# Two groups of transposes become one, ahead of a tile's scores: attention and soft-dispatch block on one core

## The reference

```python
q = rope(jnp.einsum('bim,mhd->bhid', x, wq))
k = rope(jnp.einsum('bim,mhd->bhid', x, wk))
v = jnp.einsum('bim,mhd->bhid', x, wv)
s = jnp.einsum('bhid,bhjd->bhij', q, k) / 128
p = jax.nn.softmax(s - 1e30 * (i < j), axis=-1)
o = jnp.einsum('bhij,bhjd->bhid', p, v)
x = layernorm(x + jnp.einsum('bhid,hdm->bim', o, wo))
x = layernorm(x + slot_ffn(x))
```

## Time and profile before

| | |
|---|---|
| median of 3 runs | 1807.03 us (1807.0 to 1810.64) |
| profiled execution, its own time | 1805.92 us |
| its span, first to last instruction | 1803.9 us |
| mean granted TensorE clock | 0.977 |
| TensorE busy | 1702.5 us, 94% |
| VectorE busy | 1439.6 us, 80% |
| ScalarE busy | 1238.1 us, 69% |
| GpSimd busy | 1132.2 us, 63% |

### The profile page before, as it was taken

How to read it: one execution, slowest core, us unless ns; L and a number is a source line. 1 busy time by engine, 2 the same in 40 slices (tenths; PEclk the granted TensorE clock), 3 DMA queues, 4 the chain that set the end, 5 groups by cost and what they waited for, 6 DMA issues and landing times. The chain is left out here.

```text
span 1803.9 us, 33428 instructions
## 1 busy us (share of the span) xinstructions
PE 1702.5 (94%) x10524; PEld 1482.8 (82%) x10524; DVE 1439.6 (80%) x2947; ACT 1238.1 (69%) x2362; POOL 1132.2 (63%) x696
## 2 busy tenths in 40 slices
PE   4999999999999999999999999999999965999997
PEld 3788888888888888888888888888888854889986
DVE  3888988897899888978998889788989955677764
ACT  2777777776777777767777777777777732565563
POOL 3556666665666666656666666666666624677775
PEclk7999999999999999999999999999999987999998
DMA  3222232223222323232223223322222212123212
GB/s 105 71 71 74 76 98 69 73 76 89 66 78 71 103 64 79 75 85 70 75 76 106 63 78 79 91 71 71 71 82 72 71 64 71 48 55 92 64 30 53
DMA packets 76678, 134.23 MB, mean 74 GB/s; under 512 B 19296, under 2 KB 45920, under 8 KB 76512
## 3 DMA queue, kind: packets, MB, share of 16 engines
q1 hardware_dynamic: 75328, 131.15, 27.1%
q10 hardware_dynamic: 1184, 1.05, 0.2%
HBM read 56.36 MB, written 8.70 MB: 36 GB/s over the span
## 5 line engine op out<-in xcount | busy, mean ns | idle before, releaser
L454 ACT ACTIVATE probs<-ps_slot,neg_max 128x640 f32<-128x640 f32 (+7 forms) x512 | 378.6, 741 | 123.9 <-DVE neg_max L540 114.5
L540 DVE CUSTOM_DVE_ANT_0 ps_slot<-ps_slot,causal 128x640 f32<-128x640 f32 (+7 forms) x512 | 387.1, 756 | 52.0 <-PE ps_slot L57 50.4
L691 PE MATMUL ps_turn<-ident,probs 128*128 128x128 f32 x2304 | 340.4, 277 | 18.5 <-DVE x_t L597 6.2
L418 POOL TENSOR_TENSOR q<-rot_q,q 128x1024 fp32r<-128x1024 f32 x64 | 153.9, 2405 | 240.5 <-ACT q L471 240.5
L691 PEld LDWEIGHTS ps_turn<-ident,probs 128*128 128x128 f32 x2304 | 256.5, 141 | 53.4 <-DVE x_t L597 7.9
L55 PE MATMUL ps_slot<-k,q 128*128 128x512 f32 (+3 forms) x768 | 283.9, 370 | 2.2 <-DVE rot_q L556 1.3
L57 PE MATMUL ps_slot<-k,q 128*128 128x512 f32 (+3 forms) x768 | 266.2, 347 | 0.0
L56 PE MATMUL ps_slot<-k,q 128*128 128x512 f32 (+3 forms) x768 | 266.1, 347 | 0.0
L410 POOL TENSOR_TENSOR swapped_q<-swapped_q,rope 128x1024 f32<-128x1024 f32 x64 | 165.7, 2589 | 76.0 <-DMA swapped_q<-unrot_q 76.0
L418 POOL TENSOR_TENSOR k<-rot_k,k 128x1024 fp32r<-128x1024 f32 x64 | 153.1, 2392 | 85.8 <-ACT k L471 84.2
L410 POOL TENSOR_TENSOR swapped_k<-swapped_k,rope 128x1024 f32<-128x1024 f32 x64 | 153.5, 2399 | 55.9 <-DMA swapped_k<-unrot_k 55.8
(11 more groups left out here) (159 smaller groups left out, 4360.0 us busy)
## 6 DMA issues: line engine op xcount, KB each, us to landing
swapped_k<-unrot_k SPq DMA_DIRECT2D x128, 256.0 KB, 3.6
swapped_q<-unrot_q SPq DMA_DIRECT2D x128, 256.0 KB, 3.7
inv_b<-inv_rows SPq DMA_DIRECT2D x64, 512.0 KB, 4.7
x_rows<-in_L_attn_x SPq DMA_DIRECT2D x8, 512.0 KB, 5.1
y_t<-y_sum SPq DMA_DIRECT2D x8, 512.0 KB, 5.1
row_b<-r_rows SPq DMA_DIRECT2D x16, 256.0 KB, 3.5
y_in<-y_t SPq DMA_DIRECT2D x7, 512.0 KB, 3.6
x_row<-in_L_attn_x SPq DMA_DIRECT2D x7, 512.0 KB, 5.1
```

Source lines behind the costliest of these rows:

```text
L418: pool.tensor_tensor(out[:, 1, :], rot[which][:, :], f32(out[:, 0, :]), ALU.subtract)\
L454: act.activation(probs_tile(t), score_tile(name, head, i), ACT.Exp, scale=-1.0, bias=neg_max[:, head.par, t:t + 1], accum_out=sums[:, head ...
L540: dve.tensor_tensor_reduce(tile, tile, causal[:, T - WIDTH[t]:T], -1.0, UNSEEN, ALU.add, ALU.min, neg_max[:, head.par, t:t + 1]).then_inc( ...
L691: last = pe.transpose(bank[:, at:at + P], probs_tile(t)[:, j * P:(j + 1) * P], ident[:, :])
```

## The change

On TensorE, turn 5a of the head before moves from behind the scores of tile 4 to ahead of them, directly behind turn 2. On VectorE, the low parts of turns 2 and 5a move ahead of the row maximum of tile 4. ScalarE's order stays as it was, and so do all waits, buffers and DMAs.

```diff
@@ VectorE, step @@
                 mul_cos_q(after)
                 invert(before)
-                rowmax("s4", head)
                 turn("2", before)
                 turn("5a", before)
+                rowmax("s4", head)
                 rowmax("s7", head)
                 turn("3", before)
                 turn("10", before)
@@ TensorE, step @@
                 weigh_high(before, (2, 3))
                 turn("2", before, ("4a", before))
+                turn("5a", before, ("7a", before))
                 if head.live():
                     pe.wait_ge(lo_made[1], head.made())
                     pe.wait_ge(lo_made[0], head.made())
                 free_slot(raw_made[1], after)
                 scores("s4", head)
-                turn("5a", before, ("7a", before))
                 free_slot(cos_made[0], after)
                 scores("s7", head)
                 turn("3", before, ("2", before))
```

## The result

The changed kernel takes 1838.66 us as the median of 6 runs (1834.31 to 1841.93), the kernel before 1808.97 us in the 6 runs beside it (1807.0 to 1810.64). The ratio is 1.0163, with a 95% interval of 1.0147 to 1.0180. The profiled execution took 1840.12 us, its span is 1838.2.

The account below looks back on a forecast made before the run. The prediction took TensorE, busy 94% of the span, to set the attention part's pace. Losses of 12.1, 13.2, 2.7 and 2.0 us, together 30.0, on a profiled 1805.92 gave 1836 us, range 1822 to 1850.

Parts of the forecast that it names:

- The new wait: TensorE, before tile 6's scores: waits for tile 4's exponential, made late by VectorE's new order; 0.67 us a step.
- The sum: Whole kernel: 12.1 + 13.2 + 2.7 + 2.0, together 30.0 us lost.
- the 51 common steps: Steps between two products of q: 18 of about 21.70 us lose 0.67 each, 33 of about 21.98 lose 0.40.
- The nine long steps: Steps of 24 us and more, around batch loads and the loop's turn: 0.3 of 0.67 us lost each.
- Three steps outside the 60: Steps outside the fourth-to-last span: each loses the full 0.67 us, together 2.0.
- What takes up part of it: TensorE's later arrival at turn 6b removes 0.27 us of waiting there, leaving net 0.40 in colliding steps.
- the wait at 6b: TensorE at turn 6b waits 0.27 us for 4b's low part, behind k's addition on VectorE; forecast to go.
- the colliding steps: Steps where GpSimd's sine product begins before VectorE's addition for k, which then ends 1.09 us after it.
- The saved switch: TensorE, one transposes-to-matmuls switch fewer: 0.09 us a step, priced at nothing; as rival 1, 1800 us, chance 0.04.
- no change: Rival 2: TensorE's other waits take up the delay, leaving 1806 us; chance 0.05.
- the rule on frequent short pauses: Rival 4: short TensorE pauses make its clock fall in each step, 76 us on top of 30, 1912 us; chance 0.03.
- rival 3: Nothing of the new wait is taken up, or VectorE falls behind in newly colliding steps: 1848 to 1854 us; chance 0.10.

Follow-up runs that it names:

- dve_only: Changed kernel with turn 5a on TensorE put back behind the scores of tile 4, so only VectorE's half of the change remains; 1857.71 us, ratio 1.0261.
- fill_split: Changed kernel with the first quarter of `weigh_split` (three matmuls) moved in front of the scores of tile 6; 1812.44 us, ratio 1.0013.
- fill_one: Kernel before the change, with a single matmul of the weighing of tiles 0 to 3 moved in front of turn 6b; ratio 0.9989.
- pe_only: Changed kernel with VectorE's order put back as before, so only TensorE's half of the change remains; 1821.55 us, ratio 1.0066.
- one_low: Changed kernel with the low part of 5a put back behind tile 4's row maximum, only that of turn 2 ahead; 1809.55 us, ratio 0.9998.

## Why the prediction was right

**The new wait** was forecast at 0.67 us a step and is 0.63 as idle time of the weight load in the step shown, 0.66 on average. That load, the first for the scores of tile 6, stands 4.12 us into the step, against 3.45 to 3.46 in most steps before. The low part of 5a took 0.59 to the next start, close to the 0.60 that was chosen over 0.69. Two kernels show that this wait sets the time: dve_only made it 0.33 longer and the steps 0.34; fill_split gave TensorE work in it, with the other engines' lists as they were, and the time came back.

**The sum** was 30.0 us; the medians differ by 29.7, the two profiled executions by 34.2. By its terms, in the traces: the 51 common steps 24.9 (forecast 12.1 + 13.2 = 25.3). The nine long steps gave 5.7 (forecast 2.7, with 0 and 6 as bounds): the four short ones with a batch to load grew by the full 0.65 to 0.7, three others by 0.1 or less, the two at the loop's turn by 0.8 and 2.1. In the last of these TensorE's matmuls show 3.80 us of idle time at the turn, with no releaser named, against 2.18 before; in the other kernels these two steps take between 25.1 and 27.0 us, so not all of the growth need be the change's. Ahead of the fourth step 3.4 us were lost. Three steps outside the 60 were forecast to have the new wait; the trace shows it in one ahead of them and in one behind. The second step, which has no such wait, alone grew by 2.4 us (20.28 to 22.68). It takes 22.5 to 24.6 in every kernel of the experiments, and these, some of them with no loss in their steps, also reach the fourth step at 92.3 to 94.2 us (90.50 before), so most of the 3.4 us is not shown to be the change's. Beside the common steps, then, the traces have 9.1 us, where 4.7 was forecast; that 30.0 comes so close to the 29.7 of the medians is in part luck. The common steps alone carry the agreement.

**What takes up part of it** came as described: the wait at 6b is gone in the colliding steps, and all common steps but one have one length. The reading of these steps was incomplete: that VectorE's line alone would set them at 22.0 was only seen in fill_one. It did not matter for the sum, since 22.37 is longer than the 22.0 that VectorE needs. The hold of GpSimd's product on the addition shows in the changed kernel too: the product ran from 740.25 to 742.64, the addition for k began at 740.73 and ended at 743.73, 1.09 after it. GpSimd's timeline:

```profile
740.25 2.39 POOL L410 TENSOR_TENSOR swapped_q<-swapped_q,rope 128x1024 f32<-128x1024 f32 x1 [0.98 <-DMA swapped_q<-unrot_q]
```

The addition took 3.00 us there; where it starts ahead of the product it takes 1.22. The Trainium skill, page "SBUF — State Buffer", section "Who interferes with whom", says that a VectorE instruction with two inputs in SBUF and a GpSimd instruction that reads SBUF exclude each other for the length of the one that came first; these rows agree (3.00 against 1.22).

**The saved switch** was priced at nothing, because q's product gates the scores of tile 7. That held: those start 1.28 into the step, as before (718.08 - 716.80 in the earlier trace rows; 735.18 - 733.90). The wait there, forecast at 0.2, is 0.14 by the matmuls (0.25 between two starts where a stream has 0.11), and no row of idle time names it.

**What the prediction left out** is that TensorE's half has a price: the scores of tile 4 come 0.43 us later to VectorE (their last matmul starts 1.03 into the step, 0.60 before). In the changed kernel the two low parts cover this; alone it costs 0.66%. The prediction asked of the moved transposes only what they wait for and whom they gate on TensorE, and not who waits for the scores that they were put ahead of.

**The rivals.** The saved switch and no change are excluded by the interval. The mean clock stayed at 1.00 over the 60 steps, with a pause of 0.63 to 0.68 in each; the rule on frequent short pauses, from the Trainium skill's page "TensorE: Matmul & The Clock Gate", section "A second HAM failure mode: psum-queue depth-cycling", did not take hold here. Of rival 3, the new collisions are real but hidden in the changed kernel: the addition for k is held by GpSimd's product in 43 of the 51 common steps, in 28 before; fill_split shows what they cost once TensorE is early enough.

## What to carry to other kernels

In an order written by hand, ask of each instruction that is moved ahead how late the one behind it may come: here 0.42 us were free and 1.02 cost a wait of 0.66 in every step. Find that slack at the last wait of the chain, on whichever engine it stands (row maximum, exponential, bank, scores of another tile), and count each engine's half of a change by itself, since two halves can cover or worsen each other. A wait that is filled on the busiest engine gives its length back only until the next engine's line becomes the longer one.

## What was not expected of the hardware

In 13 steps of the kernel before (738.82 us is one) the row maximum of tile 4 started 1.41 to 1.43 us into the step instead of 1.25, and turns 3 and 10 then waited for low parts. In pe_only the same steps had 1.85 to 1.87 instead of 1.50. They recur every 16 steps, which is the length of the loop; that suggests that they hang on the place in the program. Where a low part stands ahead of that row maximum, in the changed kernel and in one_low, no step shows it. No trace names the cause, and it stays open.
